# A graph network of four layers on one core: the attention blocks rewritten, and the sheaf layer relieved of half the edge lines

## The reference, cut to what matters

```python
w_m = (efeat @ W_msg + b_msg).reshape(E, in_f, -1)      # 16 x 16 per edge
w_a = (efeat @ W_attn + b_attn).reshape(E, in_f, -1)
h_src = feat[src][:, :, None]
e1 = w_m * h_src
e2 = w_a * h_src
seg_max = jax.ops.segment_max(e2, dst, num_segments=N)
ex = jnp.exp(e2 - seg_max[dst])
denom = jax.ops.segment_sum(ex, dst, num_segments=N)
attn = ex / denom[dst]
ft = jax.ops.segment_sum(e1 * attn, dst, num_segments=N)
return ft.sum(axis=1)
```

## Time and profile before

| | us |
|---|---|
| median of 3 runs | 10059.73 |
| lowest and highest run | 10047.99 and 10061.47 |
| profiled execution, first to last instruction | 13003.9 |
| of it sheaf blocks, about | 5150 to 9200 |
| of it attention blocks, about | 9340 to 12895 |

### The profile page before, as it was taken

One profiled execution on the slowest core, in us unless ns is written; L12 is line 12 of the kernel. 1 busy time (PEld: TensorE's weight loads), 2 busy tenths in 40 slices (PEclk: granted clock), 3 DMA queues, 4 the chain that ended last, 5 costly groups with the idle time before them and its releaser, 6 DMA issues. The chain is left out here.

```text
span 13003.9 us, 142499 instructions
## 1 busy us (share of the span) xinstructions
PE 8950.8 (69%) x38162; PEld 4441.1 (34%) x38162; DVE 8219.9 (63%) x14849; ACT 2527.0 (19%) x4281; POOL 6780.0 (52%) x6455
## 2 busy tenths in 40 slices
PE   2776773777777771666666666666488888888885
PEld 2333431333333330333333333334233333333332
DVE  7444442555555552555555555566488988889888
ACT  7443441111011010111111111111011111111112
POOL 0554554334443435444444444444377777777775
PEclk9887885777766765777777777778688888888887
DMA  1111111111111101100010000000122222222223
GB/s 69 41 44 38 41 42 21 26 27 25 27 27 25 26 23 15 19 19 17 19 19 19 18 19 18 18 18 12 23 65 65 65 65 65 65 66 68 65 65 107
DMA packets 495922, 492.95 MB, mean 38 GB/s; under 512 B 179009, under 2 KB 394840, under 8 KB 494937
## 3 DMA queue, kind: packets, MB, share of 16 engines
q1 hardware_dynamic: 298201, 371.17, 8.7%
q0 software_dynamic: 197504, 119.78, 6.0%
HBM read 240.53 MB, written 249.95 MB: 38 GB/s over the span
## 5 line engine op out<-in xcount | busy, mean ns | idle before, releaser
L1688 PE MATMUL sheaf_acc<-sheaf_hot_hi,sheaf_wide 128*128 128x392 bf16 x9672 | 2145.8, 376 | 1144.1 <-issue 627.8
L1608 POOL DMA_INDIRECT sheaf_got<-tab,sheaf_idx x1612 | 1664.6, 1033 | 2091.5 <-DVEq L1969 1607.4
L2127 POOL DMA_INDIRECT attn_got<-tab,attn_line x1760 | 2393.3, 1360 | 604.2 <-issue 557.4
L2186 PE MATMUL attn_q<-attn_X,ident 128*128 128x512 f32 x3520 | 1835.0, 681 | 9.3 <-DVE attn_X L2356 8.6
L1688 PEld LDWEIGHTS sheaf_acc<-sheaf_hot_hi,sheaf_wide 128*128 128x128 bf16 x9672 | 1015.4, 113 | 2062.4 <-issue 1668.0
L1862 DVE TENSOR_SCALAR sheaf_hot_hi<-sheaf_number,src_hi 128x784 bf16<-128x784 f16 x1612 | 684.7, 425 | 1421.8 <-remote 1125.8
L2178 PE MATMUL attn_w<-src_hi 32*128 32x512 f32 x3520 | 1120.8, 826 | 524.1 <-ACT src_hi L2234 317.7
L1213 POOL DMA_INDIRECT nnconv_got<-tab,nnconv_idx x1116 | 1058.2, 948 | 370.3 <-issue 322.2
L2281 DVE TENSOR_TENSOR attn_T<-attn_w,attn_got 128x1024 f32<-128x1024 f32 x880 | 1055.4, 1220 | 247.3 <-DMA attn_got<-tab,attn_line 175.3
L2186 PEld LDWEIGHTS attn_q<-attn_X,ident 128*128 128x128 f32 x3520 | 767.7, 225 | 1019.9 <-issue 1019.9
L788 PE MATMUL gcn_acc<-gcn_hot,pieces 128*128 128x512 bf16 x3906 | 974.9, 403 | 96.1 <-issue 91.5
(11 more groups left out here) (444 smaller groups left out, 12592.1 us busy)
## 6 DMA issues: line engine op xcount, KB each, us to landing
states<-attn_S SPq DMA_DIRECT2D x110, 1024.0 KB, 4.2
states<-attn_S SPq DMA_DIRECT2D x110, 512.0 KB
attn_got<-tab,attn_line POOLq DMA_INDIRECT x1760
sheaf_got<-tab,sheaf_idx POOLq DMA_INDIRECT x1612
gcn_key<-src_key SPq DMA_DIRECT2D x62, 384.0 KB
gcn_blk<-src_blk SPq DMA_DIRECT2D x62, 384.0 KB
nnconv_got<-tab,nnconv_idx POOLq DMA_INDIRECT x1116
nnconv_key<-src_key SPq DMA_DIRECT2D x62, 256.0 KB
```

The source lines that it names most:

```text
L1608: e.indirect_dma_start(out=got[at.b][:, j, D:D + T2], out_offset=None, in_=tab[2], in_offset=indices(idx[at.b], j)).then_inc(s_got[j // JH ...
L1688: mm = e.matmul(pacc[k][:, 0:HH], wide[at.b][half][:, part, col, :], hot_hi[(at.b * J + j) % NR][:, k * HH:(k + 1) * HH], start=False, sto ...
L2127: e.indirect_dma_start(out=got[at.b][:, 4 * q + n, :], out_offset=None, in_=tab[3], in_offset=indices(ids[:, q, n, :], D + 2)).then_inc(s_ ...
L2186: mm = e.matmul(pq[q % 2][:, :], ident[:, :], X[:, q, n, :], start=n == 0, stop=n == 3)
```

## The change

In the sheaf layer the gathers of lines, their marks, numbers and stores are taken out, and `quad_lines` with them. In the attention layer POOL gathers all four lines of a block; the four gathers of the next block now stand in the middle of `sources`, between its eighth and ninth gather. `T` has a new layout, and DVE's `tensor_tensor` instructions become `scalar_tensor_tensor` with the scalar 1 (`joined`). The subtractions, exponentials and products go quad by quad. The four `sums` of DVE are gone: PE adds the carried state with a fifth matmul per quad, whose weights are a diagonal matrix that ACT makes (`diagonals`), and ACT copies the result out of PSUM (`taken`). PE's order is rewritten, with the first quad's `matrices` two blocks ahead.

```diff
-    quad_lines = dram("quad_lines", (NQ, 4 * RW))
...
-                    def lines(at):
-                        if at.k >= 2:
-                            turn_wait(e, s_at, at.of(1, -1))
-                            turn_wait(e, s_lst[at.b], at.half(16, 0))
-                        for m in range(2):
-                            for q in range(NP2):
-                                e.indirect_dma_start(out=line[at.b][:, m, q, :, :].rearrange("p n f -> p (n f)"), out_offset=None,
-                                                     in_=a["lines"], in_offset=indices(line_at[at.b][:, m, :], q)
-                                                     ).then_inc(s_ln[at.b], 16)
...
-                    def step(at):
-                        sources(at)
-                        if 0 < at.k <= NBL:
-                            ids_of(at.plus(-1))
-                        if at.k < NBL:
-                            lines(at)
-
-                    walk(e, NB, step, head=2, tail=8)
+                    walk(e, NB, sources, head=2)
...
-                        if at.k < NBL:
-                            fixed(at)
                         half_step(at, 0)
                         sums(at)
...
                     hold(At(2))
-                    walk(e, NB, step, ch, 2 * 29 + 4, head=2, tail=10)
+                    walk(e, NB, step, ch, 2 * 29 + 4, head=2, tail=4)
                     e.wait_ge(s_acc, NB * J + NR)
...
-                            if q == NP2:
-                                turn_wait(e, s_ids, at.of(1, 1))
+                            if q == QB // 2 and at.k < NBQ - 1:
+                                lines(at.plus(1))
                             for n in range(4):
                                 e.indirect_dma_start(out=got[at.b][:, 4 * q + n, :], out_offset=None, in_=tab[3],
                                                      in_offset=indices(ids[:, q, n, :], D + 2)).then_inc(s_got[at.b], 16)
@@ -2134,19 +2057,18 @@
                             turn_wait(e, s_turn, at.of(1, -1))
                             turn_wait(e, s_mk, at.of(1, -1))
                         turn_wait(e, s_at, at.of(1, 1))
-                        for q in range(NP2):
-                            e.indirect_dma_start(out=line[at.b][:, NP2 + q, :, :].rearrange("p n f -> p (n f)"), out_offset=None,
+                        for q in range(QB):
+                            e.indirect_dma_start(out=line[at.b][:, q, :, :].rearrange("p n f -> p (n f)"), out_offset=None,
                                                  in_=a["lines"], in_offset=indices(line_at[at.b], q)).then_inc(s_ln[at.b], 16)
                     def ids_of(at):
-                        turn_wait(e, s_ln[at.b], at.half(16 * NP2, 16 * NP2))
-                        ids = line[at.b].bitcast(I32)[:, NP2:, :, D + 2]
-                        e.tensor_tensor(ids, ids, void_src[:, bass.ds(at.of(QB, NP2), NP2), :], ALU.add).then_inc(s_ids, 1)
+                        turn_wait(e, s_ln[at.b], at.half(16 * QB, 16 * QB))
+                        ids = line[at.b].bitcast(I32)[:, :, :, D + 2]
+                        e.tensor_tensor(ids, ids, void_src[:, at.cols(QB), :], ALU.add).then_inc(s_ids, 1)
                     def step(at):
                         sources(at)
                         if at.k < NBQ - 1:
-                            lines(at.plus(1))
                             ids_of(at.plus(1))
                     lines(At(0))
@@ -2159,7 +2081,6 @@
                     def turned(at):
-                        turn_wait(e, s_line[at.b], at.half(16, 16))
                         turn_wait(e, s_mk, at.of(1, 1))
                         turn_wait(e, s_ids, at.of(1, 1))
...
                     def quad_sum(at, q):
-                        turn_wait(e, s_prod, at.of(2, q // 2 + 1))
+                        turn_wait(e, s_prod, at.of(QB, q + 1))
                         turn_wait(e, s_taken, at.of(QB, q + 1))
                         for n in range(4):
-                            mm = e.matmul(pq[q % 2][:, :], ident[:, :], X[:, q, n, :], start=n == 0, stop=n == 3)
-                        mm.then_inc(s_quad, 1)
-
...
+                        turn_wait(e, s_diag, at.of(QB, q + 1))
+                        if q == 0:
+                            turn_wait(e, s_carried, at.of(1, 1))
+                        else:
+                            turn_wait(e, s_taken, at.of(QB, q + 2))
+                        e.matmul(pq[q % 2][:, :], diag[at.b][:, q, :], carried[:, :] if q == 0 else S[at.b][:, q - 1, CH:],
+                                 start=False, stop=True).then_inc(s_quad, 1)
                     def step(at):
-                        quad_matrices(at.plus(1), 0)
-                        quad_sums(at.plus(-1), 0)
-                        for q in range(1, QB):
-                            quad_matrices(at.plus(1), q)
-                        if at.k < NBQ - 2:
-                            turned(at.plus(2))
-                        quad_sums(at.plus(-1), 1)
+                        prev, nxt, then = at.plus(-1), at.plus(1), at.plus(2)
+                        before, more, further = at.k > 0, at.k < NBQ - 1, at.k < NBQ - 2
+                        if before:
+                            quad_sum(prev, 0)
+                            quad_sum(prev, 1)
+                        if more:
+                            matrices(nxt, 1, 0)
+                            matrices(nxt, 1, 1)
+                        if before:
+                            quad_sum(prev, 2)
+                        if more:
+                            matrices(nxt, 2, 0)
+                            matrices(nxt, 2, 1)
+                            matrices(nxt, 3, 0)
+                        if before:
+                            quad_sum(prev, 3)
+                        if more:
+                            matrices(nxt, 3, 1)
+                        if further:
+                            turned(then)
+                            matrices(then, 0, 0, 1)
                     turned(At(0))
                     for q in range(QB):
-                        for half in range(2):
-                            matrices(At(0), q, half)
+                        matrices(At(0), q, 0, 1)
                     turned(At(1))
+                    matrices(At(1), 0, 0, 1)
                     walk(e, NBQ, step, head=2)
                     for q in range(QB):
...
-                        e.copy(line_at[at.b][:, :], edges_of[:, bass.ds(at.of(QB, NP2), NP2)]).then_inc(s_at, 1)
+                            e.wait_ge(s_ln[at.b], at.half(16 * QB, 0))
+                        e.copy(line_at[at.b][:, :], edges_of[:, at.cols(QB)]).then_inc(s_at, 1)
...
                         e.copy(efT[at.b].rearrange("p q n -> p (q n)"), pturn[:, :]).then_inc(s_ef, 1)
+                    def diagonals(at):
+
+                        for q in range(QB):
+                            if q == 0 and at.k >= 2:
+                                e.wait_ge(s_quad, at.of(QB, -QB))
+                            e.activation(diag[at.b][:, q, :], ident[:, :], ACT.Copy,
+                                         scale=same_q[:, bass.ds(at.of(QB, q), 1)]).then_inc(s_diag, 1)
+
+                    def taken(at, q):
+
+                        if q == 0 and at.k >= 2:
+                            e.wait_ge(s_sc[at.b], at.half(16, 0))
+                        e.wait_ge(s_quad, at.of(QB, q + 1))
+                        e.copy(S[at.b][:, q, CH:], pq[q % 2][:, :]).then_inc(s_taken, 1)
+
+                    def exponentials(at, q):
+
+                        e.wait_ge(s_sub, at.of(QB, q + 1))
+                        if at.k > 0:
+                            e.wait_ge(s_quad, at.of(QB, q + 1 - QB))
+                        e.activation(X[:, q, :, 0:CH], T[at.b][:, q, 0, :, :], ACT.Exp).then_inc(s_x, 1)
+
                     def step(at):
+                        prev, before = at.plus(-1), at.k > 0
+                        if before:
+                            taken(prev, 0)
+                            taken(prev, 1)
+                        diagonals(at)
+                        if before:
+                            taken(prev, 2)
                         if at.k < NBQ - 2:
                             marks(at.plus(2))
-                        for n, half in enumerate(halves):
...
-                            e.wait_ge(s_sub, at.of(2, n + 1))
-                            if at.k > 0:
-                                e.wait_ge(s_quad, at.of(QB, QB // 2 * (n + 1) - QB))
-                            e.activation(X[:, half, :, 0:CH], T[at.b][:, half, :, 0:CH], ACT.Exp).then_inc(s_x, 1)
+                        for q in range(2):
+                            exponentials(at, q)
+                        if before:
+                            taken(prev, 3)
+                        for q in range(2, QB):
+                            exponentials(at, q)
                         e.wait_ge(s_e, at.of(1, 1))
```

(63 more changed lines are left out.)

143 lines of the change are left out of this document (36 added, 107 removed).

## The result

| | us |
|---|---|
| before, median of 4 runs | 10059.15 (10047.99 to 10061.47) |
| after, median of 4 runs | 11436.34 (11434.08 to 11442.04) |
| ratio after/before | 1.1372, 95% interval 1.1356 to 1.1388 |
| profiled execution after, its own time and its span | 11435.73 and 11434.0 |

The change makes the kernel 1377 us slower; 1176 were forecast. More than all of it is in the attention layer. By its long span the profile of before came from such a chip, and the one of after did not: spans of the two are not to be subtracted, single rows and the attention's periods are. The period of before on a faster chip was not profiled; by subtraction from the run with the move and the early copy it is the same (see there).

The account below looks back on a forecast made before the run. POOL was taken to set attention's pace at 31.7 of 32.15 us a block. After the change a 43.7 us loop through the late copy adds 1236 us, sheaf takes off 60: 11236 us, range 10600 to 11600.

Parts of the forecast that it names:

- The loop and its place: Attention: line gathers moved into `sources` wait for ACT's late `line_index`, closing a once-a-block loop of 43.7 us against 32.15.
- DVE and ACT on the path: Attention loop: DVE's work from landing to `drop` 16.7 us, ACT from exponential to copy 2.2 us.
- POOL and landing: Attention loop: twelve DMAs at 1.25 us plus 2.3 for holding, 17.3 together, then 1.7 us to land.
- The rule of the Trainium skill: It infers `tensor_tensor` does not stall descriptor generation; by it the 2.3 us of holding vanish, total 246 us lower.
- Waits for PE: Attention loop: DVE waits 0.4 us for the second quad's weights, the rest for the third's; 5.8 us in all.
- the low clock: PE after long idleness in attention: slower matmuls add 0 to 6 us to DVE's wait; 2.7 taken.
- The total: Whole kernel: 107 attention blocks x 11.55 = +1236 us, sheaf layer -60, giving 11236 us.
- POOL's wait and the busy shares: Attention: POOL idle some 11 to 14 us a block at the first line gather; DVE busy about 65%.
- The form of instruction: DVE's `scalar_tensor_tensor` for `tensor_tensor`: same 2.02 us at 1792 elements, both hold a gather; nothing gained or lost.
- the term of 60 us: Sheaf layer's gain, 1.1 us x 55 blocks, bounds 22 and 473; the profile's longer blocks were put down to recording.
- sheaf gains as in the profile: Rival: sheaf layer gives back 413 us more, as its profiled blocks suggest; 10823 us, chance 10%.
- The rivals with a timely copy: Attention, copy not late: block 29.0 us, 9656 us total, 4%; or POOL bound at 32.6, 10049 us, 3%.

## Why the prediction was right, step by step

- **The loop and its place** were right, and the gathers moved ahead of a late copy are shown to be the main cause: the early copy alone takes back 1191 us, the move alone puts 12.0 us a block on the kernel before, the move with the early copy takes 1.4 off.
- **DVE and ACT on the path**: forecast 16.7 + 2.2 = 18.9 us. From 9005.82 to 9032.96 are 27.14 us, less the stops 0.42, 6.24 and 1.69: 18.8.
- **POOL and landing**: forecast 17.3 + 1.7 = 19.0; from 9032.96 to 9052.00 are 19.04. The first three line gathers, under two-operand work of DVE, took 1.45, 1.43 and 1.90 us: 1.9 us of being held, forecast 2.3. The copy was followed by 0.82 us before the first gather where I had a pause of 0.30: two small misses that cancel. The rule of the Trainium skill that the forecast weighed (SBUF — State Buffer, "Who interferes with whom") is again not borne out: in the kernel with move and early copy, whose DVE uses `tensor_tensor`, the source gathers take 1.33 us in the mean, and 0.94 when nothing holds one. Whether the writing of descriptors is held or another part of the gather, no run shows.
- **Waits for PE** were the mis-sized term: 5.8 us forecast, 7.3 us in the mean (763.7/104), 8.35 in the block shown. For the third quad's weights I had 2.7 for the order and 2.7 for the low clock, and the wait was 6.24: the clock stayed low for some 4.7 us of the third `quad_sum`'s 5.98 (granted clock 0.61 in that window). With the `matrices` ahead of it, 3.60 us where they take 1.14 at full clock, the low clock costs 2.5 + 2.3 = 4.7 us by the rows (an estimate), where I let it rise part of the way through and took 2.7. The 1.69 us before the last `times`, for weights that stand behind the fourth `quad_sum`, was missing in the sum. In the run with the early copy, without the low clock, the third quad's wait was 2.42 us, near the 2.7 that I gave to the order alone; but there DVE had stood 3.93 us for the second quad's weights, so that the two are not quite alike.
- **The total**: 45.06 in place of 43.7 us a block and 109 blocks in place of 107 make +1408 for +1236. The sheaf layer gave back 53 us, forecast 60. The remaining 20 or so us lie between the stages and are not explained.
- **POOL's wait and the busy shares** were read off wrongly, though the sum was not: POOL stood 17.5 us at the line gathers where I named 11 to 14, and DVE's share is 57% for about 65%. The 11 fit a POOL block of 32.6 us, with about 7 us of holding as before the change; the holding is 2.0 us at the line gathers (4 x 1.445 less 4 x 0.945) and next to nothing at the source gathers (0.949 us in the mean).
- **The form of instruction** was worth nothing, as said; what DVE's lighter work is worth was not tested alone. Two more DMAs cost 2.54 us in place of 2.5 where their landing is not hidden.
- **A wrong reason**: the profile of before is long because of its chip, not because of the recording. That the term of 60 us came out near 53 is luck: it was taken near the busy-time end for a wrong reason, and holds because the runs of the result were on a faster chip. On the other kind of chip the rival "sheaf gains as in the profile" is the true one (322 to 393 us, forecast 473 at most), and the whole change costs 1060 us.
- **The rivals with a timely copy** had the wrong bound. POOL was put at 32.6 us, DVE at 29.0. It came to 34.16, set by DVE's work and 8.1 us of waits for PE where I allowed 2.9. So the change would have been a loss of 1.9% even with its copy in time. Whether some order of PE leaves fewer waits stays open: the one that was tried left more.

## What to carry to other kernels

Before a step is moved earlier in a queue, list what it waits for and who makes that, and move the maker too: here the copy had been ready 7.8 us before its reader, and after the move the reader stood 17.5 us for it. Moving that one copy of 0.19 us to the head of ACT's step took back most of the loss. Where two engines feed each other by turns, add their waits to their work before naming a third as the next bound. And before a long profile is put down to recording, compare its own time with runs on the same chip.

## What the runs showed of the hardware

- The same kernel took 10,059 to 10,061 us on two chips and 13,018 to 13,036 on two others. On the latter PE's signals can come some 10 us late by the record (9.9 us above), while DVE's and ACT's instructions and POOL's unheld gathers have their usual lengths (1.22, 0.59 and 0.94 us). The first three of the four layers are longer there (sheaf rows of before: 4076.4 us against 2613.3), and the attention of the kernel before, which POOL binds, is not (32.12 us on both kinds, on the faster one by subtraction). That the late signals are the whole difference between the chips is not shown.
- DVE's two-operand work holds POOL's own small instruction too: `ids_of` took 2.05 us in the mean where it lies beside the products, and 0.21 us in the kernel before.
- An idle time of 4.55 us of PE was followed by the low clock (granted 0.54 in the next 9.7 us) just as one of 7.97 was (0.56).
